# Two-layer attention and expert kernel: paired value products, masked maxima on VectorE, outputs kept transposed, one-piece scratch reads, combine weights repeated by DMA

## The chip, the cores and the metric

One Trainium2 chip, one core. The metric is the device time of one execution in microseconds; the kernel before takes 1240.22 us (median of 3 runs, 1240.1 to 1241.93).

## The reference, cut to what matters

```python
x = L0_attn_x                                   # (1, 1024, 256) float32
xn = _layernorm(x)
s = _L0_attn_ref(xn, ...)                       # differential attention
g = _silu(_L0_ffn_ref(xn, weight, bias))        # MXFP4-rounded x and weight
x = x + s * g
xn = _layernorm(x)
s = _L1_attn_ref(xn, ...)                       # causal attention, 16 heads of 16
g = _silu(_L1_ffn_ref(xn, ...))                 # 16 experts of 176 rows, top 4, and shared rows
x = x + s * g

# L0 attention: 16 heads, 4 key/value heads, two halves of 16
q1, q2 = rope(q halves); k1, k2 = rope(k halves), repeated 4 times
a1 = softmax(q1 k1 / 4 + causal mask); a2 = softmax(q2 k2 / 4 + causal mask)
out = (a1 - lam * a2) @ v                       # v is 32 wide
out = (out - mean) * rsqrt(var + EPS)           # over tokens and the head's 32 columns
out = (out * gn_w + gn_b) * 0.8 @ Wo
# L1 experts
h1 = xt @ W1[e].T; h3 = xt @ W3[e].T
y = sum_e (silu(h1) * h3 * combine[:, e]) @ W2[e].T
```

## The kernel before

Five blocks follow each other, each ended by a barrier of all engines: the setup (lines 175 to 362), the attention of layer 0 (`attention(0, ...)`, L365), `middle` (L798), the attention of layer 1, and `experts` (L1137). All addresses, semaphores and orders are written out by hand; each engine runs its own list in order.

**Setup.** x is normalised, transposed and multiplied by the query and key weights in ten units of 128 rows by 512 tokens (`UN`, L161; keys first). Each unit is rotated (rope) and split into three bf16 parts by ScalarE, VectorE and GpSimd into `spl`, a ring of 4 units; the SP queue writes it to a scratch in DRAM (L221), and `stacked0` (L164) reads it back in six transfers of 16 partitions each, one per pairing of a part of q with a part of k, so that `stack0` holds 96 rows that a single bf16 product contracts. Three more rows hold the row maxima in bf16 parts.

**Attention.** A head, or in layer 1 two heads, is called a pair: 16 pairs in layer 0, 8 in layer 1, each of 24 blocks. For every block TensorE makes three products:
- the max step (L447): scores of 128 queries against up to 512 keys. On the diagonal a second product adds the mask (L451): 16 of the 24. VectorE takes the row maximum out of PSUM (L577, L580). It runs `LEAD` = 38 blocks ahead through a ring of 3 banks.
- the score step (L460): scores of 128 keys against up to 512 queries with the maxima subtracted, into one of `AHEAD` = 2 banks; ScalarE takes the exponential (L535) into `pr`, a ring of 4; GpSimd clears the triangle on the diagonal (L710, 16 of 24).
- the value step (L480): float32, 64 columns of the array in layer 0 and 32 in layer 1. Half m = 0 and half m = 1 of a block pair go to different columns and partitions of one bank. It trails by one block: `value_step(n - 1)`.

The widths (`SB`, L46, and `MB`, L57) add up to 9216 columns in a pair for each of the three. The last column of each value operand is ones, so the sum of the exponentials comes out beside the output. Finished outputs of a pair and 512 tokens are copied by ScalarE (L544), turned by four float32 products with `sel` (L500), copied again (L551), and normalised by VectorE and GpSimd (L598, L690 to L702). SP brings the maxima of the next pair into `stack` (L729), the late units, and in layer 1 the expert weights (L737, L740). In layer 0 VectorE also runs the MXFP4 rounding (L605), one piece of 256 columns per pair in ten pairs.

**Middle.** Group statistics of the layer 0 output, gain and offset (L968, L969), four transposes a tile (L1056), Wo, gate, residual, second norm, transposes, value and router products, then eight projection units of layer 1, split, written and gathered as in the setup (L849, L775), the routing, and the combine weights as three bf16 parts.

**Experts.** 50 units (25 tiles of 128 expert rows, twice for 512 tokens each): 12 products for the two hidden layers (L1237), one with a one-hot matrix that repeats the combine weights over the rows (L1244), ScalarE, VectorE (L1374, L1377, L1383), GpSimd (L1332, L1347, L1351), and two units later 6 products down (L1257). Ahead of them the layer 1 output is transposed (L1212) and multiplied by Wo (L1221); after them eight tiles are transposed back (L1277), gated and stored one by one (L1324, L1389, L1392, L1356, L1202).

## Time and profile before

| | us |
|---|---|
| median of 3 runs | 1240.22 |
| span of the profiled execution (its own time lies about 1.8 above the span, if it is like the median) | 1238.4 |
| TensorE matmul busy | 1135.3 (92%) |
| VectorE busy | 556.6 (45%) |
| ScalarE busy | 478.6 (39%) |
| GpSimd busy | 420.3 (34%) |
| TensorE weight load busy | 496.2 (40%) |

Busy matmul time is modelled and overlaps at its ends, so costs of TensorE are read from one start to the next. "Granted clock" is the share of 2.4 GHz at which TensorE was allowed to run; its two levels are 1.0 (2.4 GHz) and 0.5 (1.2 GHz). PEld is the weight load.

### The profile page before, as it was taken

Reading aid. Unit: us, or ns where it says so; the run is one execution under the profiler, and the core shown is the slowest. Engines: PE = TensorE matmul, PEld = TensorE weight load, DVE = VectorE, ACT = ScalarE, POOL = GpSimd, SP = SyncE. Lnnn points to the kernel's source line nnn. Section 1 sums busy time; section 2 is a strip of 40 time slices with the busy share of each in tenths; the row PEclk is TensorE's granted clock in tenths of the full one; section 3 lists DMA queues with packets and bytes.
Section 4 is the critical chain, followed back from the end, with each engine's and each line's share of the span. In section 5 each row is a group of like instructions: output and inputs, shape, how many; then the busy total and the mean of one; then the engine's idle time right before and its main releaser. Section 6 shows DMA issues by size and latency. Waiting matters only on the chain. (4 is left out here: it accounts for less than half of the span.)

```text
span 1238.4 us, 14306 instructions
## 1 busy us (share of the span) xinstructions
PE 1135.3 (92%) x4490; PEld 496.2 (40%) x4490; DVE 556.6 (45%) x1198; ACT 478.6 (39%) x981; POOL 420.3 (34%) x863
## 2 busy tenths in 40 slices
PE   5559999999999999999797299999999799999996
PEld 2322333333333333333374123222322377777774
DVE  3564555555555444440366264444440044444444
ACT  2313444444444444444223124444444344444443
POOL 2612222222222222222322111222222267767774
PEclk9969999999999999999788679999999899999998
DMA  4755310000000000000103855111111000000001
GB/s 147 146 101 72 47 20 1 1 1 1 1 1 1 1 1 1 1 1 1 30 0 64 141 91 91 40 40 41 40 40 43 24 1 0 0 1 0 0 0 35
DMA packets 32226, 39.24 MB, mean 32 GB/s; under 512 B 5386, under 2 KB 24427, under 8 KB 32158
## 3 DMA queue, kind: packets, MB, share of 16 engines
q1 hardware_dynamic: 32164, 38.48, 15.5%
q8 instruction: 31, 0.51, 0.2%
q14 instruction: 31, 0.25, 0.1%
HBM read 30.05 MB, written 8.13 MB: 31 GB/s over the span
## 5 line engine op out<-in xcount | busy, mean ns | idle before, releaser
L480 PE MATMUL ps<-top,mid 128*64 128x512 f32 (+3 forms) x768 | 330.5, 513 | 0.0
L535 ACT ACTIVATE top<-ps 128x512 f32<-128x512 f32 (+3 forms) x384 | 188.6, 491 | 280.7 <-PE ps L460 280.5
L447 PE MATMUL ps<-mid 96*128 96x512 bf16 (+3 forms) x576 | 194.3, 346 | 46.6 <-DMA mid<-part_scratch 41.3
L580 DVE TENSOR_REDUCE top<-ps 128x1 f32<-128x512 f32 (+3 forms) x256 | 148.7, 587 | 113.0 <-PE ps L447 74.4
L460 PE MATMUL ps<-mid 99*128 99x512 bf16 (+3 forms) x576 | 194.6, 339 | 0.5 <-ACT mid L535 0.3
L460 PEld LDWEIGHTS ps<-mid 99*128 99x128 bf16 x576 | 57.6, 100 | 311.4 <-ACT top L535 191.1
L710 POOL TENSOR_SCALAR_AFFINE_SELECT top<-top 128x128 f32<-128x128 f32 x256 | 74.8, 292 | 251.5 <-ACT top L535 251.5
L480 PE MATMUL ps<-mid 128*32 128x512 f32 (+3 forms) x384 | 159.8, 500 | 0.0
L535 ACT ACTIVATE mid<-ps 128x512 f32<-128x512 f32 (+1 forms) x192 | 94.0, 490 | 152.0 <-PE ps L460 151.5
L1237 PE MATMUL ps<-xp,wp 128*128 128x512 f32 (+1 forms) x600 | 144.7, 390 | 0.0
L1237 PEld LDWEIGHTS ps<-xp,wp 128*128 128x128 f32 (+1 forms) x600 | 111.9, 187 | 24.9 <-issue 0.5
L480 PEld LDWEIGHTS ps<-top,mid 128*64 128x64 f32 x768 | 73.4, 135 | 91.2 <-issue 72.3
L580 DVE TENSOR_REDUCE mid<-ps 128x1 f32<-128x512 f32 (+3 forms) x128 | 73.8, 590 | 55.3 <-PE ps L447 33.8
L577 DVE TENSOR_REDUCE top<-ps 128x1 f32<-128x128 f32 (+3 forms) x128 | 61.1, 483 | 72.1 <-PE ps L451 72.1
L451 PE MATMUL ps<-keep 128*128 128x128 bf16 x384 | 88.2, 230 | 0.0
L1374 DVE SCALAR_TENSOR_TENSOR a<-th,ps 128x512 f32<-128x512 f32 (+1 forms) x50 | 34.4, 687 | 115.5 <-ACT th L1303 115.5
L1332 POOL TENSOR_TENSOR wp<-top,wp 128x512 fp32r<-128x512 f32 (+1 forms) x50 | 64.7, 1295 | 61.7 <-ACT wp L1288 61.7
L1257 PE MATMUL ps<-gp,w2p 128*128 128x512 f32 (+1 forms) x300 | 82.6, 411 | 1.5 <-POOL gp L1351 1.5
L447 PEld LDWEIGHTS ps<-mid 96*128 96x128 bf16 x576 | 58.6, 102 | 62.4 <-issue 42.6
L710 POOL TENSOR_SCALAR_AFFINE_SELECT mid<-mid 128x128 f32<-128x128 f32 x128 | 37.4, 292 | 131.5 <-ACT mid L535 131.5
L1351 POOL TENSOR_TENSOR gp<-g,gp 128x512 fp32r<-128x512 f32 (+1 forms) x50 | 64.1, 1283 | 17.1 <-ACT gp L1316 17.0
L1257 PEld LDWEIGHTS ps<-gp,w2p 128*128 128x128 f32 (+1 forms) x300 | 52.5, 188 | 21.7 <-issue 9.3
(204 smaller groups left out, 1055.7 us busy)
## 6 DMA issues: line engine op xcount, KB each, us to landing
mid<-part_scratch SPq DMA_DIRECT2D x54, 256.0 KB, 9.3
part_scratch<-top SPq DMA_DIRECT2D x18, 384.0 KB, 11.4
top<-in_w SPq DMA_DIRECT2D x16, 396.0 KB, 4.0
top<-in_w SPq DMA_DIRECT2D x8, 384.0 KB, 4.8
keep<-in_x SPq DMA_DIRECT2D x1, 1024.0 KB, 5.8
top<-in_rope SPq DMA_DIRECT2D x1, 1024.0 KB, 7.7
out<-gg SPq DMA_DIRECT2D x8, 128.0 KB, 1.7
mid<-top SPq DMA_DIRECT2D x48, 4.0 KB, 1.7
```

The lines of the kernel that those rows point to most:

```text
L447: ins = nc.tensor.matmul(bank[:, 0:w], queries(pair, m)[0:PARTS, i * P:(i + 1) * P], keys(pair, m)[0:PARTS, c * 512:c * 512 + w], start=Tr ...
L451: ins = nc.tensor.matmul(bank[:, w - P:w], idb[:, :], mkb[:, :], start=False, stop=True)
L460: nc.tensor.matmul(ps[:, ST_BANK + n % AHEAD, 0:w], keys(pair, m)[0:STACK, j * P:(j + 1) * P], queries(pair, m)[0:STACK, q0:q0 + w], start ...
L480: nc.tensor.matmul(ps[r0:r0 + rw, ACC + c, q0 - 512 * c:512], v, pr[:, n % 4, 0:w], start=start, stop=stop).then_inc(multiplied, 1)
L535: nc.scalar.activation(pr[:, n % 4, 0:w], ps[:, ST_BANK + n % AHEAD, 0:w], ACT.Exp, scale=0.25).then_inc(p_ready, 1)
L577: ins = nc.vector.tensor_reduce(nm[:, pair % 2, m, i:i + 1], bank, AX.X, ALU.max, negate=True)
L580: ins = nc.vector.tensor_reduce(mx[:, m, i - 4, c:c + 1], bank, AX.X, ALU.max)
L710: nc.gpsimd.affine_select(out=square, in_=square, pattern=[[1, P]], compare_op=ALU.is_ge, fill=0.0, base=0, channel_multiplier=-1).then_in ...
L1237: last = nc.tensor.matmul(ps[0:r, bank + b, :], wp[:, b, pw, w + kk, 0:r], xp[:, px, kk, c * 512:(c + 1) * 512], start=j == 0 and kk == 0, ...
L1257: last = nc.tensor.matmul(ps[:, YB + kk, :], w2p[0:r, b, pw, kk * P:(kk + 1) * P], gp[0:r, b, pg, :], start=first and j == 0, stop=final a ...
L1332: nc.gpsimd.tensor_tensor(wp[:, b, 1, :, 0:r], w13[:, :, :, bass.ds(i * P, r)].rearrange("p w c n -> p (w c) n"), wp[:, b, 0, :, 0:r].bitc ...
L1351: nc.gpsimd.tensor_tensor(gp[0:r, b, 1, :], g[0:r, b, :], gp[0:r, b, 0, :].bitcast(F32), ALU.subtract).then_inc(gl_ok, 1)
```

## The change

What it does, by place (line numbers with "after" are those of the changed kernel):
- Value steps are issued in groups: the two halves of a block together (`GROUPS`, 12 groups in a pair in layer 0), in layer 1 from block 8 on four together, each on its own 32 columns. The rings grow: 3 score banks, `pr` of 8.
- The mask product is gone. VectorE adds the mask and takes the maximum in one operation that also writes the masked scores back to PSUM, with the maximum read out by a second small instruction (L709 after).
- The products with `sel` and their copies are gone. Outputs stay transposed in `oT`: SP moves them from the copied bank into `oT` (halves apart in layer 0) and the sums of exponentials into `cd` (L435 after); for every four pairs VectorE inverts, SP writes the inverses to DRAM and reads them repeated, GpSimd multiplies, VectorE combines the halves and takes statistics.
- The scratch holds each unit six times in the order of the stack, written in three transfers, and is read in one transfer of 96 partitions, the first two maps of a group ahead of the other six. `spl` has 8 units.
- MXFP4 runs in five pieces of 512 columns, six of eleven steps on GpSimd.
- Middle: no transposes of the output; gain and offset act on `oT` in place; the bias row is bf16 in three parts; units in another order; combine weights go to DRAM in float32.
- Experts: no transposes ahead, no one-hot product; two DMAs a unit repeat rows of the combine weights; Wo products run inside the sweep; tiles 0 to 3 are turned and gated inside the sweep; the last copy is shared by two engines.

```diff
-                S_RING, AHEAD = 3, 2
+                RING, LAG = 8, 1
+                GROUPS = [(b, b + 2) for b in range(0, 8 if not first else PAIR, 2)]
+                if not first:
+                    GROUPS += [(b, b + 4) for b in range(8, PAIR, 4)]
+                GROUP_AT = {(hi + LAG) % PAIR: (lo, hi) for lo, hi in GROUPS}
+                S_RING, AHEAD = 3, 3
...
-                            if diag:
-                                ins = nc.tensor.matmul(bank[:, w - P:w], idb[:, :], mkb[:, :], start=False, stop=True)
...
-                            if n > 0:
-                                value_step(n - 1)
...
-                            if out_number(n) >= 0:
-                                sel_step(out_number(n), pair + 1)
+                            if k in GROUP_AT and n > LAG:
+                                lo, hi = GROUP_AT[k]
+                                for done in range(n - LAG - (hi - lo), n - LAG):
+                                    value_step(done)
...
+                            if c == i // 4:
+                                low = i < 4
+                                to = nm[:, pair % 2, m, i:i + 1] if low else mx[:, m, i - 4, c:c + 1]
+                                ins = nc.vector.tensor_tensor_reduce(
+                                    bank, bank, msk[:, 512 - w:512], -1.0 if low else 1.0,
+                                    3e38 if low else -3e38, ALU.add, ALU.min if low else ALU.max, to)
```

```diff
-            for n, j in enumerate(KPARTS if f == 4 else QPARTS):
-                sp.dma_start(stack0[16 * n:16 * n + 16, base:base + 8, :],
-                             scr[j, f * P:(f + 1) * P, :].rearrange("(m r) t -> r m t", r=16)).then_inc(stk0[f], 16)
+            sp.dma_start(stack[0:PARTS, at + lo:at + hi, :],
+                         of[f * P + 16 * lo:f * P + 16 * hi, :, :].rearrange("(m r) n t -> (r n) m t", r=16)
+                         ).then_inc(done, 16)
...
+            def outputs(sp, pair, c):
...
+                    for m, to in ((0, o1[32 * h:32 * h + 32, f, columns(c)]), (1, second(f)[32 * h:32 * h + 32, c, :])):
+                        at, row = 64 * m, 16 * (2 * h + m)
+                        sp.dma_start(to, src[at:at + 32, :]).then_inc(outs[c], 16)
+                        sp.dma_start(cd[row:row + 16, c, 0, :], src[at + 32:at + 33, :]).then_inc(outs[c], 16)
...
+            def scale(pool, f, c):
...
+                pool.wait_ge(inv_r[c], READS * (f + 1))
+                if first:
+                    n1, rd = second(f)[:, c, :], repeated(c)
+                    nc.gpsimd.tensor_tensor(n1, n1, rd[1], ALU.mult)
+                    nc.gpsimd.tensor_tensor(to, to, rd[0], ALU.mult).then_inc(scaled, 1)
...
+                        for pair in range(N):
+                            if pair > 0:
+                                outputs(sp, pair - 1, 1)
+                            if f > 0 and h == 0:
+                                inverses(sp, f - 1, 0)
+                            if pair + 1 < N:
+                                ahead(pair + 1)
+                            outputs(sp, pair, 0)
+                            if f > 0 and h == 0:
+                                inverses(sp, f - 1, 1)
...
-                    nc.tensor.matmul(ps[0:r, CB + b, :], ones[:, bass.ds(i * P, r)], combT(c),
-                                     start=True, stop=True).then_inc(c_ok, 1)
...
+                    if c == 0 and isinstance(i, int) and 3 <= i < 4:
+                        for q in range(2):
+                            through_wo(q)
```

How the order moves, at two places. TensorE in layer 0, from the middle of a pair on; L447 is the max step, L451 the mask, L480 the value step, L460 the score step. Before:

```order
L447 MATMUL ps<-mid 128x512
L451 MATMUL ps<-keep 128x128
L480 MATMUL ps<-top,mid 64x512
L460 MATMUL ps<-mid 128x512
L447 MATMUL ps<-mid 128x128
L451 MATMUL ps<-keep 128x128
L480 MATMUL ps<-top,mid 64x512
L460 MATMUL ps<-mid 128x512
L447 MATMUL ps<-mid 128x128
```

and now, where L622 is the score step, L605 the max step and L642 the value step ("x2" is two in a row):

```order
L622 MATMUL ps<-mid 128x512
L605 MATMUL ps<-mid 128x128
L622 MATMUL ps<-mid 128x512
L605 MATMUL ps<-mid 128x128
L642 MATMUL ps<-top,mid 33x512 x2
L622 MATMUL ps<-mid 128x512
L605 MATMUL ps<-mid 128x256
```

Two value products now stand together behind two score and two max steps, and the mask products are gone.

VectorE in layer 0, now (L709 is the masked maximum and its read-out, L713 the plain maximum, L717 the join of the halves, L725 the copy of the maxima rows):

```order
L713 TENSOR_REDUCE top<-ps 128x1
L709 ISA ps,top<-ps,keep 128x512
L709 ISA top 128x1
L717 TENSOR_REDUCE top<-top 128x2x4
L709 ISA ps,top<-ps,keep 128x128
L709 ISA top 128x1
L709 ISA ps,top<-ps,keep 128x128
L709 ISA top 128x1
L709 ISA ps,top<-ps,keep 128x256
L709 ISA top 128x1
```

Sixteen of the 24 maxima of a pair became two instructions each, of which the first has two inputs and writes a whole block.

## Rows read from the trace of the kernel before

**Rows 1.** Stretches: us, busy PE, PEld, DVE, ACT, POOL, granted clock, DMA share, GB/s.
```profile
72.00:93.00 21.00, 16.94 (x73) 6.91 (x73) 18.16 (x41) 1.58 (x3) 1.63 (x7) 0.66 0.32 75
93.00:603.00 510.00, 507.58 (x1993) 167.82 (x1991) 231.58 (x533) 210.09 (x445) 134.65 (x441) 1.00 0.07 9
604.00:706.00 102.00, 68.66 (x274) 43.90 (x275) 51.00 (x168) 25.62 (x55) 26.89 (x33) 0.75 0.38 65
706.00:727.00 21.00, 17.88 (x74) 7.16 (x74) 18.49 (x41) 1.88 (x4) 1.75 (x7) 0.58 0.29 60
727.00:970.00 243.00, 242.94 (x951) 70.66 (x951) 91.32 (x183) 102.57 (x220) 50.88 (x183) 1.00 0.22 52
```

**Rows 2.** TensorE in layer 0, in order of time: start, us, line, shape.
```profile
281.07 0.22 PE L447 MATMUL ps<-mid 96*128 96x128 bf16 x1
281.13 0.22 PE L451 MATMUL ps<-keep 128*128 128x128 bf16 x1
281.27 0.86 PE L480 MATMUL ps<-top,mid 128*64 128x384 f32 x2
282.07 0.23 PE L460 MATMUL ps<-mid 99*128 99x128 bf16 x1
...
283.51 0.65 PE L480 MATMUL ps<-top,mid 128*64 128x256 f32 x2
```

**Rows 3.** Groups of the other engines and of the `sel` products: busy us, mean ns.
```profile
L535 ACT ACTIVATE top<-ps 128x512 f32<-128x512 f32 (+3 forms) x384 | 188.6, 491 | 280.7 <-PE ps L460 280.5
L500 PE MATMUL ps<-keep,top 128*128 128x66 f32 x256 | 35.4, 281 | 0.7 <-ACT top L544 0.7
L241 POOL TENSOR_TENSOR top<-top 128x512 f32<-128x512 f32 x10 | 14.5, 1452 | 15.1 <-DVE top L315 15.1
```

**Rows 4.** TensorE at the end of each attention, where two value products meet.
```profile
598.24 0.65 PE L480 MATMUL ps<-top,mid 128*64 128x256 f32 x4
...
968.74 0.63 PE L480 MATMUL ps<-mid 128*32 128x256 f32 x4
```

**Rows 5.** VectorE, in order of time: a maximum and what follows it; two operations with PSUM.
```profile
280.05 0.69 DVE L580 TENSOR_REDUCE top<-ps 128x1 f32<-128x512 f32 x1 [0.74 <-PE ps L447]
280.65 0.41 DVE L637 TENSOR_TENSOR top<-top 128x256 f32<-128x256 f32 x1
...
995.71 0.69 DVE L1374 SCALAR_TENSOR_TENSOR a<-th,ps 128x512 f32<-128x512 f32 x1 [2.70 <-ACT th L1303]
996.43 0.69 DVE L1377 TENSOR_TENSOR a<-a,ps 128x512 f32<-128x512 f32 x1
```

**Rows 6.** Waits for scratch, in order of time; then GB/s in 40 slices: gathers, unit writes.
```profile
59.62 0.62 ACT L270 CAST top<-top 128x512 bf16<-128x512 f32 x1 [11.78 <-DMA part_scratch<-top]
72.24 0.26 PE L447 MATMUL ps<-mid 96*128 96x128 bf16 x1 [19.64 <-DMA mid<-part_scratch]
705.91 0.27 PE L447 MATMUL ps<-mid 96*128 96x128 bf16 x1 [21.63 <-DMA mid<-part_scratch]
GB/s 0 0 7 7 7 92 266 120 113 126 130 109 102 137 109 106 113 157 109 109 113 140 92 99 157 109 41 0 27 0 0 0 0 0 0 0 0 0 0 0
GB/s 0 0 0 0 0 106 352 357 337 357 313 29 0 0 0 0 0 0 0 0 5 299 357 337 357 337 159 0 0 0 0 0 0 0 255 352 352 347 347 198
```

**Rows 7.** TensorE in the experts, in order of time: Wo, first hidden products, one whole unit.
```profile
982.13 10.14 PE L1221 MATMUL ps<-wo_s,oT 128*128 128x256 f32 x32 [6.97 <-DMA onehot_s<-in_onehot]
...
998.56 3.02 PE L1237 MATMUL ps<-xp,wp 128*128 128x512 f32 x12
...
1003.32 2.88 PE L1237 MATMUL ps<-xp,wp 128*128 128x512 f32 x12
1006.13 0.39 PE L1244 MATMUL ps<-keep,onehot_s 51*128 51x512 bf16 x1
1006.45 1.66 PE L1257 MATMUL ps<-gp,w2p 128*128 128x512 f32 x6
1007.95 0.39 PE L1237 MATMUL ps<-xp,wp 128*128 128x512 f32 x1
```

More of the change, by code:

```diff
@@ new lines, in program, with unit_written, written @@
+        unit_near = sem("unit_near")
+        scr_ok = [sem(f"scr_{n}") for n in range(SLOTS)]
+        def unit_written(layer, v):
+            slot = v % SLOTS
+            before = len(range(slot, len(UN), SLOTS)) if layer == 1 else 0
+            return scr_ok[slot], 48 * (before + v // SLOTS + 1)
+        UN = [(f, c) for f in (4, 0, 1, 2, 3) for c in range(NC)]
+        UN1 = [(2, 0), (0, 0), (2, 1), (0, 1), (3, 0), (1, 0), (3, 1), (1, 1)]
+        def written(sp, to, f, c, parts, is_key, done):
+            rows = to[f * P:(f + 1) * P, :, c * 512:(c + 1) * 512]
+            for first_row, width, part in ((0, 3, 0), (3, 2, 1), (5, 1, 2)):
+                if is_key:
+                    of = parts[:, part, :].unsqueeze(1).to_broadcast([P, width, 512])
+                else:
+                    of = parts[:, 0:width, :]
+                sp.dma_start(rows[:, first_row:first_row + width, :], of).then_inc(done, 16)
@@ new lines, in attention @@
+            o_evac = sem(f"o_evac{layer}")
+            outs = [sem(f"outs{layer}_{c}") for c in range(NC)]
+            inv, inv_w, scaled = (sem(f"{n}{layer}") for n in ("inv", "inv_w", "scaled"))
+            inv_r = [sem(f"inv_r{layer}_{c}") for c in range(NC)]
+            combined = sem("combined0") if first else scaled
+            if not first:
+                den_sum, num_sum = sem("den_sum"), sem("num_sum")
+            PER = (64, 64) if first else (64, 128)
+            READS = 32 if first else 16
@@ L649, in _ @@
                             pair, k = divmod(n, PAIR)
+                            f, h = divmod(pair, 4)
                             if n + LEAD < BLOCKS:
@@ L741, in weights, with ahead @@
                                          ).then_inc(ld_m, 16)
-                        for pair in range(N):
+                        def ahead(pair):
                             rows(pair)
@@ L1069, in _, with ffn @@
                 last.then_inc(q_tr, 1)
-                for n, part in enumerate((pm, pq)):
+                pe.wait_ge(q_ev, 3)
+                pe.wait_ge(bip_ok, 2)
+                def ffn(t):
+                    z = ps[:, 4 + t // 2, (t % 2) * D:(t % 2 + 1) * D]
+                    for k in range(KD):
+                        nc.tensor.matmul(z, aT[:, k, t * P:(t + 1) * P], wT[:, k, :], start=k == 0, stop=False)
+                    for j in range(3):
+                        last = nc.tensor.matmul(z, row[:, :], bip[:, j, :], start=False, stop=j == 2)
+                    last.then_inc(f_mm, 1)
@@ L1071, in _, with total @@
+                def total(n):
                     pe.wait_ge(stats, n + 1)
-                    nc.tensor.matmul(ps[:, 7, 16 * n:16 * n + 16], share[:, :], part[:, :], start=True,
+                    nc.tensor.matmul(ps[:, 3, 4 * n:4 * n + 4], share[:, :], (pm, pq)[n][:, :], start=True,
                                      stop=True).then_inc(tot, 1)
+                for t in range(NT):
+                    ffn(t)
+                    if t >= 6:
+                        total(t - 6)
                 def values(t):
-                    pe.wait_ge(ldw, 64)
@@ L1222, in _, with back @@
                                                     wo1[:, k, :], start=k == 0, stop=k == KD - 1)
                     last.then_inc(s_mm, 1)
-                pe.wait_ge(xl_ok, 1)
+                def back(t, bank, at):
+                    for k in range(KD):
+                        last = nc.tensor.transpose(ps[:, bank, at + k * P:at + (k + 1) * P],
+                                                   yT[:, t // 4, k, (t % 4) * P:(t % 4 + 1) * P], idf[:, :])
+                    last.then_inc(z_ok, 1)
```

973 lines of the change are left out of this document (553 added, 420 removed).

## The prediction

> **What bounds the kernel now.** I read the busy time by stretches first, to see which engine fills which stage. In both steady attention stretches TensorE is full: 507.58 of 510 us and 242.94 of 243 us, at granted clock 1.00, with VectorE at 45% and 38% [rows 1]. So 753 of 1238 us cost what TensorE's instructions cost. The two short stretches ahead of them (21 us each) belong to VectorE: it is busy 18.2 and 18.5 us there, and the clock is 0.66 and 0.58. The middle has TensorE at 67%.
>
> Next I read TensorE's instructions in order, from one start to the next. A max product of 128 columns takes 0.06 us (281.07 to 281.13), the mask product behind it and the switch to the value product 0.14, so a mask costs about 0.07. A value product of 384 columns takes 0.80 to the next score product (281.27 to 282.07) [rows 2]. At 2.4 GHz one bf16 pass is 384/2400 = 0.16 us; 0.80 is 384/600 = 0.64 plus 0.16. With the 0.08 on its front, a value product costs w/600 us and 0.245 us fixed. Each kind of product has 9216 columns and 24 instructions a pair:
>
> - value 15.36 + 24 x 0.245 = 21.2 us
> - score 3.84 + 24 x 0.01 = 4.1; max 4.1; 16 masks 1.1
> - `sel`: 35.4 us busy for 16 pairs, 2.2 each [rows 3]
>
> Sum 32.7; measured 510/16 = 31.9, so the model is right to 3%.
>
> **Side by side.** At the end of the layer 0 attention two value products of 256 columns that have nothing between them, one per half of the array, lie in one group that lasts 0.65 us; in layer 1, on 32 columns each, 0.63 [rows 4]. One product alone of the same width lasts 0.65 [rows 2]. So two cost one; that they do is no hope but a row. That four cost one is shown by no row. I take it, since layer 1 shows two products on quarter tiles; if four cost two rounds, that is a bound below.
>
> Layer 0 after: values 7.68 + 12 x 0.245 = 10.7 (a group costs its fixed part once), score 4.1, max 4.1: 18.9 a pair, 302 in all, less 38 max products that run in the stretch ahead (6 us): 296. Layer 1: four groups of two (512, 384, 256, 128 columns: 0.853 + 0.640 + 0.427 + 0.213) and four groups of four (3 x 0.853 + 0.427) are 5.1 us, with 8 x 0.245 = 7.1; with score and max 15.3 a pair, 122 in all, less 6: 116.
>
> **Who could be late instead.** ScalarE: 24 exponentials at 0.491 are 11.8 us a pair by duration [rows 3], and two copies make some 13, less from start to start. GpSimd: all its work in layer 0 is 134.65/16 = 8.4 a pair [rows 1]; the scaling adds, each four pairs, 4 operations of 1.45 [rows 3], 1.5 a pair. VectorE: a maximum of 512 columns takes 0.60 from start to start and 0.69 by duration [rows 5]; all 24 are w/960 + 0.07 each, 11.3 a pair. The masked maximum is on no row. Bounds: nothing more than a plain maximum (it reads the same bank), or 0.6 more at 512 (as if adding and taking the maximum were two passes). The nearest rows are operations of the same engine with PSUM on one side and 512 elements of output, 0.69 each, 0.72 when the second depends on the first [rows 5]; with the read-out behind it I take 0.2 more per masked block: 11.3 + 3.2 = 14.5. That is below 18.9 in layer 0 and just below 15.3 in layer 1.
>
> So layer 0 keeps TensorE as its bound with 77% for VectorE there; I add 12 us for MXFP4 pieces of 512 columns on VectorE and steps of GpSimd among its triangles, a stall of 0.5 to 1 us a pair. Layer 1 has three engines within 20%; rows of maxima that SP brings while the next max products are already due add some 0.7 to 1 us a pair, and uneven load 3 to 5: 14 in all. Both stretches ahead, 38 maxima with VectorE as bound, grow by about 38 x 0.13 = 5 us each. Sums: layer 0 from 508 (its 510 and the last steps) to 308, -200; layer 1 from 243 to 130, -113.
>
> **Start.** ScalarE stood 11.78 us for the ring of 4 units, TensorE 19.64 us for the gather, which moved 102 to 126 GB/s, while unit writes move 350 [rows 6]. The ring of 8 takes the first wait; the read in one transfer of 96 partitions and the near maps first take most of the second. The scratch is written twice as large (six copies for three): at 350 GB/s a unit of 786 KB needs 2.2 us, about one unit's pace of GpSimd (2.8). I put the first max product at 56.5 for 72.24: -15.7. If the wide read gave nothing, +10.
> The Trainium skill (page "SBUF — State Buffer", on how partitions reach the DMA ports) says that a transfer confined to partitions 0 to 15 reaches 4 ports and measured 104 GB/s. By that rule, the gathers of before agree with it (102 to 126), and a transfer of 96 partitions should not be held so.
>
> **Middle.** TensorE's wait of 21.63 before layer 1 [rows 6] shrinks to some 5, for the same reasons and by the order of the units: -17. Four transposes and their copies for each of eight tiles go, -7, the rest of the tile loop stays. Sum -24; -14 to -32 as bounds.
>
> **Experts.** Before: the first hidden products of the second unit at 998.56, 28.6 us after the last value product; a unit takes 4.63 us (1003.32 to 1007.95), of which the one-hot product has 0.32 (1006.13 to 1006.45), 0.55 with its two switches [rows 7]. I take 0.42 x 50 = -21. The transposes ahead and the wait for the one-hot matrix (6.97 us) go, the inverses of the last heads, their trip through DRAM and the scaling now stand before Wo but not before the hidden products: -9. Wo takes 10.14 us there, partly at half clock; inside the sweep 8: +8. The last tiles, four turned inside the sweep at 1.1 each: -4.6. Two issues of SP per unit, within 4.2 us, cost nothing while both land in time: each reads one row of 2 KB and writes 128 partitions. If they don't, a unit waits (+1 here; up to +20 as bound). Sum -25.5.
>
> **Sum**, against the profiled execution: 1238.4 - 15.7 + 5 - 200 - 24 + 5 - 113 - 25.5 = 870, and 1.8 for what lies around the span (the median stands 1.8 above it): **871 us**. Of the 368 us saved, 310 are the value products, `sel` and masks.
>
> **Rivals.**
> (a) VectorE sets the pace. The masked maximum costs its upper bound (0.6 more at 512, 0.37 on average, and the read-out): 17.3 us or more a pair. Layer 1 then follows it (+16 to +20), layer 0, where VectorE has MXFP4 too, +10, both stretches ahead +8 each: about 915. TensorE would then idle a tenth of layer 1, and the rows say what idling can do: in the stretches where it waits between products its granted clock is 0.58 and 0.66 [rows 1]. At 1.2 GHz layer 1's 15.3 us become some 25, +80 less what VectorE costs anyway: up to 950. For it: 14.5 against 15.3 is close. Chance 0.14.
> (b) Four cost two rounds, or the products meet only in part because operands come late: layer 1 pays 3 x 0.853 + 0.427 again, +3 us a pair, 24 in all: 895. This lies inside the likeliest range, so it is counted there.
> (c) Products keep strict turns. A float32 product is two instructions on the trace; if the first of a neighbour could not start before the second of the other had started, only one pass in three would be shared. A pair of layer 0 would take 3/4 of the old value time instead of half, +3.84 x 16 = 61; in layer 1 five passes for eight instead of two, +5.5 x 8 = 44: 976. [Rows 4] speak against it: x4 in 0.65 us, not 0.97. Chance 0.04.
> The Trainium skill (page "TensorE: Matmul & The Clock Gate", Part 3, on packing small matmuls) states that matmuls start and end strictly in program order. By that rule two neighbours of two passes would share one pass only, which is this rival; the trace speaks against it.
> (d) The value products don't meet at all in the steady state (both halves share a bank and a stationary load that blocks): only the switches are saved. +7.7 x 16 and +10 x 8 come back: about 1075. Chance 0.03.
> (e) Slower than before: the masked maximum, one instruction with two inputs and a written block, is dear. VectorE would need (1240 - 360)/24, over 34 us a pair where it now needs 11.3, so 1.8 us for an average masked block of 320 columns. No row comes near: 0.69 for 512, and even GpSimd's 1.45 for 512 would give about 970. Chance 0.01. That the change does not do what it says I can exclude but for such costs: the new order shows the products next to each other.
>
> **How the numbers follow.** My forecast (TensorE sets the pace, both widths side by side) has 0.78 with its own range of 832 to 905; its spread is +-12 for start and middle, -15 to +24 for layer 1, +-15 for layer 0 stalls, -12 to +20 for the experts, which don't all fall to one side. (a) 0.14 at 905 to 950, (c) 0.04 at 976, (d) 0.03 at 1075, (e) 0.01. A range of 832 to 950 leaves out (c), (d), (e) and an edge of the first. A difference under 0.2%, 2.5 us, can't be told from none for this kernel; all cases but (e) are far beyond it. Faster 0.985, same 0.005, slower 0.01.
>
> **What would show it.** First max product near 56; stretches ahead 26 us each with VectorE full; layer 0's steady part 308 us with TensorE over 90% busy at clock 1.00, VectorE 77%; groups of value products 0.86 us for 512 columns in x4, and x8 in layer 1; the masked maximum at 0.7 to 0.9 us for 512; middle 78 us; layer 1 130 us; experts 243. Wrong if masked maxima last over 1.1 us, if TensorE waits mostly for VectorE (a), if x4 groups last 1.3 (c) or 1.7 (d), if x8 lasts 1.7 (b), or if the granted clock leaves 1.00 in either attention.

## The result and the profile after

The changed kernel takes **868.4 us** (median of 4 runs, 865.64 to 868.93) against 1240.16 us in the same comparison: ratio 0.6998, 95% interval 0.6986 to 0.701. The forecast was 871, its range 832 to 950. The profiled execution has a span of 867.2 us.

The first view is again the stretches, now of the changed kernel, with cuts at the first max product, the first score product and the last value product of each layer. Columns: us, busy PE, PEld, DVE, ACT, POOL, granted clock, DMA share, GB/s.

```profile
0.00:63.70 63.70, 34.36 (x108) 18.16 (x109) 29.57 (x63) 21.33 (x38) 30.34 (x30) 0.94 0.64 200
63.70:82.00 18.30, 14.62 (x39) 4.23 (x40) 17.48 (x65) 0.00 (x0) 0.96 (x6) 0.50 0.22 67
82.00:375.00 293.00, 291.70 (x1514) 84.02 (x1512) 209.42 (x653) 184.92 (x415) 133.77 (x358) 0.99 0.19 47
375.00:470.50 95.50, 60.71 (x248) 37.95 (x249) 40.51 (x152) 24.45 (x51) 22.37 (x35) 0.76 0.38 106
470.50:488.80 18.30, 14.63 (x39) 4.22 (x40) 17.49 (x65) 0.00 (x0) 1.10 (x6) 0.50 0.28 92
488.80:623.00 134.20, 126.14 (x738) 35.79 (x736) 88.00 (x277) 88.60 (x207) 46.13 (x159) 0.94 0.40 112
623.00:867.00 244.00, 220.75 (x950) 180.61 (x948) 126.95 (x170) 112.99 (x211) 195.92 (x160) 0.94 0.22 63
```

With the kernel before cut at the same events (72.2, 90.3, 599.2, 705.9, 724.0 and 969.7 us), the forecast can be set beside the measured change stage by stage:

| stage | before | after | change | forecast |
|---|---|---|---|---|
| start to first max product | 72.2 | 63.7 | -8.5 | -15.7 |
| stretch ahead, layer 0 | 18.1 | 18.2 | +0.1 | +5 |
| layer 0, first score to last value | 508.9 | 292.9 | -216.0 | -200 |
| middle | 106.7 | 95.8 | -10.9 | -24 |
| stretch ahead, layer 1 | 18.1 | 18.2 | +0.1 | +5 |
| layer 1 | 245.7 | 134.0 | -111.7 | -113 |
| experts | 268.7 | 244.5 | -24.2 | -25.5 |
| sum | 1238.4 | 867.2 | -371.2 | -368 |

The sum was right to 3 us, but five of the seven terms were not: the start and the middle gave 20 us less than forecast, VectorE's two stretches and layer 0 gave 26 us more. That the total came so close was partly luck; the two large terms, the layers with 313 of the 368 us forecast, were read from the right rows.

The next rows are in order of time: two value products of 512 columns and their neighbours in layer 0, then four in layer 1. "x4" is two products of two passes, "x8" four.

```profile
372.09 0.34 PE L622 MATMUL ps<-mid 99*128 99x256 bf16 x2
372.36 1.05 PE L642 MATMUL ps<-top,mid 128*33 128x512 f32 x4
373.34 0.23 PE L622 MATMUL ps<-mid 99*128 99x128 bf16 x1
...
619.50 0.28 PE L622 MATMUL ps<-mid 99*128 99x256 bf16 x1
619.71 1.05 PE L642 MATMUL ps<-mid 128*17 128x512 f32 x8
620.70 0.34 PE L622 MATMUL ps<-mid 99*128 99x256 bf16 x2
```

Both groups last 1.05 us, and the next score product comes 0.98 and 0.99 us after their start. By the w/600 of the prediction the 512 columns of one product, in its two passes, are 0.853 us. So two products cost one, as [rows 4] had shown, and four cost one too, which no row had shown. In the group of four the first passes start within 0.02 us of each other, at 619.71 to 619.73, and the second passes 0.44 us later. The four extra weight loads are hidden as well.

VectorE at the start of the stretch ahead, where it sets the pace (L709 is the masked maximum, its second row the read-out):

```profile
64.24 0.33 DVE L709 CUSTOM_DVE_ANT_0 ps<-ps,keep 128x128 f32<-128x128 f32 x1
64.48 0.14 DVE L709 DVE_READ_ACCUMULATOR2_ANT top<- 128x1 f32 x1
64.48 0.47 DVE L709 CUSTOM_DVE_ANT_0 ps<-ps,keep 128x256 f32<-128x256 f32 x1
...
66.28 0.73 DVE L709 CUSTOM_DVE_ANT_0 ps<-ps,keep 128x512 f32<-128x512 f32 x1
66.93 0.73 DVE L709 CUSTOM_DVE_ANT_0 ps<-ps,keep 128x512 f32<-128x512 f32 x1
67.58 0.69 DVE L713 TENSOR_REDUCE top<-ps 128x1 f32<-128x512 f32 x1
```

A masked maximum of 512 columns takes 0.65 us from start to start (66.28 to 66.93) against 0.60 for a plain one in [rows 5]. The read-out runs inside the next instruction. The first eight maxima, two of each width, take 3.56 us (64.02 to 67.58); in the kernel before the same eight, plain, took 3.45:

```profile
706.32 3.53 DVE L577 TENSOR_REDUCE mid<-ps 128x1 f32<-128x128 f32 x8 [14.26 <-PE ps L451]
709.77 1.48 DVE L580 TENSOR_REDUCE mid<-ps 128x1 f32<-128x512 f32 x3
```

So the mask costs VectorE 0.01 to 0.05 us a block, where 0.2 was taken. (The eight plain ones are from the stretch ahead of layer 1; ahead of layer 0 they take 3.44.)

### The profile page after: what moved, and what is told of

The parts are those of the page before. It is cut to its first block and busy times, and to the rows that moved or that the text cites. A ratio compares the mean times of both kernels' runs of the same rounds, so it can differ in the third digit from the quotient of the medians.

```text
span 867.2 us, 12855 instructions
## 1 busy us (share of the span) xinstructions
PE 762.9 (88%) x3632; PEld 365.0 (42%) x3632; DVE 529.4 (61%) x1441; ACT 432.3 (50%) x922; POOL 430.6 (50%) x751
## 5 line engine op out<-in xcount | busy, mean ns | idle before, releaser
L675 ACT ACTIVATE top<-ps 128x512 f32<-128x512 f32 (+3 forms) x384 | 171.0, 490 | 132.4 <-PE ps L622 132.2
L605 PE MATMUL ps<-mid 96*128 96x512 bf16 (+3 forms) x576 | 191.2, 356 | 29.0 <-PEq L981 11.8
L709 DVE CUSTOM_DVE_ANT_0 ps<-ps,keep 128x512 f32<-128x512 f32 (+3 forms) x384 | 184.2, 504 | 41.9 <-PE ps L605 41.2
L622 PE MATMUL ps<-mid 99*128 99x512 bf16 (+3 forms) x576 | 185.7, 338 | 9.2 <-ACT mid L675 6.3
L642 PE MATMUL ps<-top,mid 128*33 128x512 f32 (+3 forms) x768 | 161.6, 500 | 0.0
L622 PEld LDWEIGHTS ps<-mid 99*128 99x128 bf16 x576 | 54.3, 99 | 185.8 <-ACT top L675 103.0
L675 ACT ACTIVATE mid<-ps 128x512 f32<-128x512 f32 (+1 forms) x192 | 82.6, 492 | 69.9 <-PE ps L622 41.8
L713 DVE TENSOR_REDUCE top<-ps 128x1 f32<-128x512 f32 x128 | 88.4, 691 | 36.0 <-PE ps L605 35.5
L605 PEld LDWEIGHTS ps<-mid 96*128 96x128 bf16 x576 | 58.2, 102 | 75.3 <-issue 30.1
L1533 ACT CAST gp<-g 128x512 fp32r<-128x512 f32 (+1 forms) x50 | 31.1, 622 | 68.3 <-DVE g L1631 68.3
L1568 POOL TENSOR_TENSOR w2p<-top,w2p 128x256 fp32r<-128x256 f32 (+1 forms) x50 | 57.5, 1151 | 2.7 <-ACT w2p L1530 2.7
L642 PE MATMUL ps<-mid 128*17 128x512 f32 (+3 forms) x384 | 55.0, 512 | 0.0
L713 DVE TENSOR_REDUCE mid<-ps 128x1 f32<-128x512 f32 x64 | 44.1, 689 | 16.2 <-PE ps L605 16.1
```

Of the source, the lines that this page charges most:

```text
L605: nc.tensor.matmul(ps[:, s_bank(turn), 0:w], queries(pair, m)[0:PARTS, i * P:(i + 1) * P], keys(pair, m)[0:PARTS, c * 512:c * 512 + w], st ...
L622: nc.tensor.matmul(ps[:, ST_BANK + n % AHEAD, 0:w], keys(pair, m)[0:STACK, j * P:(j + 1) * P], queries(pair, m)[0:STACK, q0:q0 + w], start ...
L642: nc.tensor.matmul(ps[r0:r0 + dv, ACC + c, q0 - 512 * c:512], v, pr[:, n % RING, 0:w], start=start, stop=stop).then_inc(multiplied, 1)
L675: nc.scalar.activation(pr[:, n % RING, 0:w], ps[:, ST_BANK + n % AHEAD, 0:w], ACT.Exp, scale=0.25).then_inc(p_ready, 1)
L709: ins = nc.vector.tensor_tensor_reduce(bank, bank, msk[:, 512 - w:512], -1.0 if low else 1.0, 3e38 if low else -3e38, ALU.add, ALU.min if ...
L713: ins = nc.vector.tensor_reduce(mx[:, m, i - 4, c:c + 1], bank, AX.X, ALU.max)
```

## Where the start and the middle lost what was forecast

The change takes ScalarE's wait for the ring of 4 away, and GpSimd has finished its last unit at 56.2 us, which is where the forecast put the first max product. It starts at 63.70. SP, in order of time:

```profile
46.37 0.82 SPq L182 DMA_DIRECT2D mid<-part_scratch  x2
47.23 15.85 SPq L178 DMA_DIRECT2D part_scratch<-top  x18
```

SP issues 18 unit writes until 63.08, 0.88 us each, and the block of the setup ends for all engines only when SP's list is done. While it does so the DMA engines are full:

```profile
52.00:56.00 4.00, 0.67 (x6) 0.47 (x5) 0.87 (x2) 2.83 (x6) 3.87 (x4) 1.00 1.07 289
56.00:60.00 4.00, 0.00 (x0) 0.00 (x0) 0.35 (x2) 0.00 (x0) 0.18 (x1) 0.55 1.09 383
60.00:64.00 4.00, 0.28 (x3) 0.31 (x4) 0.00 (x0) 0.00 (x0) 0.26 (x2) 0.50 1.09 384
```

The same stands at the end of the middle: 12 writes issued from 456.60 on take SP 13.03 us, and TensorE waits 11.76 us for the end of the block. Besides, the outputs' last part costs more there than the transposes gave back: the tile loop starts 28.8 us after the block's first product (378.83 to 407.67), for 19.6 before, since the inverses of the last heads go through DRAM first: GpSimd waits for them until 396.86. Without the transposes a tile then takes 2.95 us from start to start for 3.74, 6.3 in eight tiles.

```profile
396.86 1.26 POOL L491 TENSOR_TENSOR top<-top 128x512 f32<-128x512 f32 x1 [12.33 <-DMA top<-inverse_scratch]
401.78 0.59 PE L1231 MATMUL ps<-top 128*128 128x4 f32 x2 [7.01 <-DVE top L1122]
...
407.67 7.27 PE L1273 MATMUL ps<-top,keep 128*128 128x256 f32 x24 [3.59 <-ACT keep L1041]
...
470.51 1.86 PE L605 MATMUL ps<-mid 96*128 96x128 bf16 x7 [11.76 <-PEq L981]
```

Two theories could explain SP's 0.88 us an issue: full DMA engines, whose queue lets SP add work only as fast as work leaves, or the issues as such. The next two runs tell them apart.

## Experiments

Ratios below are to the kernel before in the same comparison, with 95% intervals; the changed kernel has 0.6986 to 0.701.

**One piece more in every unit write.**

```diff
-            for first_row, width, part in ((0, 3, 0), (3, 2, 1), (5, 1, 2)):
+            for first_row, width, part in ((0, 2, 0), (2, 1, 0), (3, 2, 1), (5, 1, 2)):
```

> The changed kernel with each unit written in four transfers for three, the same bytes. If DMA bandwidth holds SP at the end of the setup and of the middle: no change in either (within 1 us). If the issues of SP do (15.85 us for 18 DMAs, 0.88 each): six units behind the gathers cost 6 x 0.88 = 5 us in the setup and about as much in the middle, 868 + 10 = 878.

Measured: 868.05 us (867.41 to 869.73), ratio 0.7001 (0.6989 to 0.7013). First max product at 64.1 for 63.7, the middle 96.1 for 95.8. SP now:

```profile
46.97 16.47 SPq L178 DMA_DIRECT2D part_scratch<-top  x24
```

24 issues in 16.47 us for 18 in 15.85: 0.69 each for 0.88. The bytes set the pace, not the issues: that is the first theory. (From run to run, with the setup unchanged, the first max product comes at 63.1 to 65.2 us, so 0.4 us there says nothing; the 18 writes take 15.6 to 16.0 in all of them.)

**The far gather behind the writes.**

```diff
                         if u == 3:
                             near_maps0(sp, 0)
-                            far_maps0(sp, 0)
+                    far_maps0(sp, 0)
```

> The changed kernel with the 1152 KB gather of the far maps of the first group issued after the last unit write of the setup instead of ahead of six of them. Theory 1 (the setup's end waits for SP, and SP for DMA bandwidth: the trace shows 380 to 385 GB/s until the barrier): 1.15 MB leave the way of the writes, the first max product comes 3 us earlier, 60.7 for 63.7, and the far maps are needed only by the second pair, some 12 us later: 865. Theory 2 (SP is held by its own issues, 0.88 us each): one issue less ahead, at most 0.9 us earlier. Rival: the second pair's first max product waits for the gather, nothing gained.

Measured: 867.57 us (866.96 to 868.54), ratio 0.6995 (0.6986 to 0.7005). The first max product comes at 62.7, 1.0 us earlier, not 3, and that is within its spread; the writes themselves are the measure:

```profile
47.41 13.98 SPq L178 DMA_DIRECT2D part_scratch<-top  x18
61.43 0.68 SPq L182 DMA_DIRECT2D mid<-part_scratch  x1
```

The writes are issued 1.7 us sooner (61.39 for 63.08), and 0.7 of it goes to issuing the gather, still inside the block. That 1.15 MB at 380 GB/s give only 1.7 us back and not 3 was missed; with the gather behind, the engines run at 366 GB/s from 52 to 56 us and 347 from 56 to 60, which would fit that GpSimd's making of units now holds the writes in part; no run tests it. A gain of 0.8 us in the median can't be told from none.

**Value steps one at a time.**

```diff
-                GROUPS = [(b, b + 2) for b in range(0, 8 if not first else PAIR, 2)]
-                if not first:
-                    GROUPS += [(b, b + 4) for b in range(8, PAIR, 4)]
+                GROUPS = [(b, b + 1) for b in range(PAIR)]
```

> The changed kernel with value steps one at a time again (24 groups of one in a pair), all else kept. Theory (products side by side save a whole block's columns and the fixed part once a group): a pair's value products go from 10.7 to 15.36 + 24 x 0.245 = 21.2 us in layer 0 (+169 over 16 pairs) and from 7.1 to 21.2 in layer 1 (+113 over 8, less the 18 us in which TensorE now waits there): 1130 to 1150 us. Rival (the gain came from masks, sel and the transposed outputs, the grouping is worth its switches alone): 868 + 24 x 3 = 940 at most.

Measured: 1115.15 us (1114.88 to 1115.42), ratio 0.8993 (0.8968 to 0.9017): 247 us given back, 15 less than the low end of what was expected. Value products, layer 0 and layer 1, with the first and last start after the comma; first of the changed kernel, then of this one:

```profile
L642 PE MATMUL ps<-top,mid x768: 272/552/1065, 85.7 to 374.7; 128*33 128x512 f32 x96, 128*33 128x384 f32 x32, 128*33 128x256 f32 x32, 128*33 128x128 f32 x32
L642 PE MATMUL ps<-mid x384: 272/546/1061, 492.5 to 622.6; 128*17 128x512 f32 x96, 128*17 128x384 f32 x32, 128*17 128x256 f32 x32, 128*17 128x128 f32 x32
```

```profile
L640 PE MATMUL ps<-top,mid x768: 272/552/1063, 85.6 to 536.9; 128*33 128x512 f32 x96, 128*33 128x384 f32 x32, 128*33 128x256 f32 x32, 128*33 128x128 f32 x32
L640 PE MATMUL ps<-mid x384: 272/546/1061, 651.8 to 870.2; 128*17 128x512 f32 x96, 128*17 128x256 f32 x33, 128*17 128x384 f32 x32, 128*17 128x128 f32 x31
```

Layer 0: 451.3 us for 289.0, +162 (169 expected). Layer 1: 218.4 for 130.1, +88, below the 95 to 113 expected. The durations of single records are the same in both kernels: nothing in a record tells that its product shares its time, only the starts do. The rival, 940 at most, is out.

**The grouping alone, in the kernel before.**

```diff
-                            if n > 0:
-                                value_step(n - 1)
+                            if n > 0 and n % 2 == 0:
+                                value_step(n - 2)
+                                value_step(n - 1)
```

with a ring of 6 for `pr` and the last two steps behind the loop.

> The kernel before with one edit: value steps two at a time, every second block, in both layers, with a ring of 6 exponentials for 4. Theory (the same sum): 10.6 us a pair less on TensorE, 24 pairs: 1240 - 254 = 986. Rival 1 (rings too short: TensorE waits for exponentials behind each group): 1020 to 1080. Rival 2 (products of two passes share one pass only): 3.84 us a pair less than that gain, 1240 - 254 + 92 = 1078.

Measured: 993.25 us (992.68 to 993.83), ratio 0.801 (0.7987 to 0.8032); 246 us less, by 254 expected. Layer 0 went from 508.9 to 339.3 us (first score to last value), 169.6 less, which is 16 x 10.6; layer 1 from 245.7 to 165.9, 80 of the 85 expected. Both rivals, short rings and one shared pass in three, are out. The value operands still have their 64 and 32 columns here, so the 33 and 17 of the changed kernel are not what the gain hangs on. This single edit is two thirds of the whole gain.

**Groups of two in all of layer 1.**

```diff
-                GROUPS = [(b, b + 2) for b in range(0, 8 if not first else PAIR, 2)]
-                if not first:
-                    GROUPS += [(b, b + 4) for b in range(8, PAIR, 4)]
+                GROUPS = [(b, b + 2) for b in range(0, PAIR, 2)]
```

> The changed kernel with groups of two in layer 1 from block 8 on as well. TensorE then needs 19.3 us a pair in layer 1 for 15.3. Theory 1 (four side by side cost one, and layer 1 now loses 18 us to waits that a slower TensorE would hide): +14 us, 882. Theory 2 (the waits add to TensorE's time whatever it does): +32, 900. Rival (four side by side cost two rounds already, or another engine sets layer 1's pace): no change.

Measured: 876.78 us (875.92 to 878.51), ratio 0.7071 (0.7053 to 0.7089): +8.4 us. Layer 1 takes 143.6 for 134.0. TensorE's own sum for it by the rule is 8 x 19.3 - 6 = 148, 4 us too much. With groups of four the rule gives 116 and the time is 134. Of these 18 us the trace gives 8.1 as idle time of TensorE (134.20 us less 126.14 busy); with groups of two it is 0.6:

```profile
488.90:632.40 143.50, 142.88 (x738) 38.11 (x736) 89.81 (x278) 91.64 (x207) 46.29 (x159) 0.98 0.37 104
```

So a slower TensorE does hide the idle time, and the rival (four already cost two rounds) is out. Theory 1 holds, at two thirds of its size. Another 7 us are the price of 14.7 us at the low clock, where groups of two have 6.5 us of it; the section on the forecast has the rows.

**The mask back on TensorE.**

```diff
+                            if diag:
+                                ins = nc.tensor.matmul(ps[:, s_bank(turn), w - P:w], idb[:, :], msk[:, 384:512], start=False, stop=True)
...
-                                ins = nc.vector.tensor_tensor_reduce(
-                                    bank, bank, msk[:, 512 - w:512], -1.0 if low else 1.0,
-                                    3e38 if low else -3e38, ALU.add, ALU.min if low else ALU.max, to)
+                                ins = nc.vector.tensor_reduce(to, bank, AX.X, ALU.max, negate=low)
```

> The changed kernel with the mask product on TensorE and plain maxima on VectorE, as in the kernel before. Theory (TensorE is the bound of both attentions, the masked maximum costs VectorE only some 0.04 us over a plain one): 16 x 0.07 = 1.1 us a pair on TensorE, 27 us over 24 pairs, and 2 to 3 us in each of the two stretches ahead, where TensorE runs at 1.2 GHz: 893 to 900. Rival (the masked maximum is dear and VectorE paces layer 1): 0.13 x 16 us a pair come back there, and the time stays within 5 us of 868.

Measured: 880.95 us (878.16 to 884.21), ratio 0.71 (0.7072 to 0.7128): +12.6, half of what was expected. Layer 0 takes 305.2 for 292.9 us. Of the 256 masks 229 lie there (27 fall on the 38 blocks that run ahead), so one costs 12.3/229 = 0.054 us, which is 128 columns at 2.4 GHz and nothing for the switch; 0.07 had been read. Layer 1 takes 2.9 us more (136.9 for 134.0) where its 101 masks would be 5.4. That its waits cover the rest is not shown: layer 1 unchanged takes 131 to 134 us from run to run. The stretches ahead stay at 18.1 and 18.7 us.

**The masked maximum alone, in the kernel before.**

```diff
-                            if diag:
-                                ins = nc.tensor.matmul(bank[:, w - P:w], idb[:, :], mkb[:, :], start=False, stop=True)
...
+                            if c == i // 4:
+                                low = i < 4
+                                to = nm[:, pair % 2, m, i:i + 1] if low else mx[:, m, i - 4, c:c + 1]
+                                ins = nc.vector.tensor_tensor_reduce(
+                                    bank, bank, msk[:, 512 - w:512], -1.0 if low else 1.0,
+                                    3e38 if low else -3e38, ALU.add, ALU.min if low else ALU.max, to)
```

> The kernel before with the mask product replaced by the masked maximum alone. Theory (TensorE is the bound, a mask costs it the 0.053 us that putting it back into the changed kernel cost): 15 masks a pair in the steady part x 24 pairs x 0.053 = 19 us less: 1221; the stretches ahead of it unchanged, since VectorE needs 0.04 us more for a block and TensorE has slack there. By the 0.07 of the prediction: 1213. Rival (dear maxima on VectorE): the steady part is unchanged and the two stretches ahead grow by 5 us each: 1250.

Measured: 1222.36 us (1219.26 to 1223.15), ratio 0.9846 (0.9829 to 0.9863): 17.7 us less, by 19 expected from 0.053 (the 19 counted 15 masks a pair; 330 lie in the two layers, 13.75 a pair, which makes 17.5). Layer 0 495.4 for 508.9, layer 1 241.1 for 245.7, both stretches ahead 18.2.

**More work on VectorE.**

```diff
                             turn = in_turn(n)
+                            for e in range(3):
+                                nc.vector.memset(idle[:, 3 * k + e, :], 0.0)
```

> The changed kernel with three memsets of 128x8 on VectorE in front of every maximum, as a stand-in for a masked maximum that is dearer (0.07 to 0.12 us each, by 32x32 memsets of 0.12 in the trace: 0.2 to 0.36 a block, 5 to 8.6 us a pair). If VectorE's slack is what the busy times say (layer 0: 13.1 of 18.3 us a pair, layer 1 in the full pairs 13.4 of 16): both stretches ahead +8 to +14 each, layer 0 +0 to +40, layer 1 +16 to +35: 895 to 960. The rival of the prediction also has TensorE's clock fall to 1.2 GHz in layer 1 when VectorE sets the pace: then layer 1 takes over 190 us. If there is more slack than busy times say, only the two stretches ahead grow: 885 to 890.

Measured: 871.13 us (870.28 to 872.0), ratio 0.7022 (0.7011 to 0.7033): +2.7. The load was too light to decide what it was meant to: three memsets cost 0.042 us a block from start to start (both stretches ahead grew from 18.2 to 19.8, 1.6 us for 38 blocks), not 0.2 to 0.36, for they overlap. Small work shows by its duration (65 ns each) more than it costs. Layer 0 (294.2) and layer 1 (132.7) stay within what they take unchanged (292.9 to 294.3 and 131 to 134), so they have at least 1 us a pair of slack on VectorE, which is what the load comes to. What a masked maximum dearer by 0.37 would have done, the clock included, stays open.

**Expert weights behind the outputs.** In layer 1 one wait stands out, in the second pair:

```profile
517.12 0.58 ACT L685 COPY mid<-ps 64x512 f32<-64x512 f32 x1 [2.48 <-DMA keep<-mid]
...
518.24 0.61 PE L622 MATMUL ps<-mid 99*128 99x512 bf16 x1 [2.76 <-ACT mid L675]
```

ScalarE's copy of a finished output waits until SP's transfers have emptied the copy's target; they had been issued from 505.95 us on, behind 1.2 MB of expert weights (504.35 to 505.91). TensorE stood 2.76 us, and its granted clock fell from 1.00 to 0.61 in the ten us around it:

```profile
515.00:525.00 10.00, 7.24 (x31) 1.71 (x29) 4.60 (x20) 4.22 (x8) 2.05 (x8) 0.61 0.15 22
525.00:535.00 10.00, 10.00 (x58) 2.98 (x56) 6.69 (x19) 5.88 (x16) 3.41 (x12) 0.88 0.38 129
```

```diff
                             rows(pair)
                             late(sp, pair)
-                            if not first:
-                                weights(pair)
...
                             outputs(sp, pair, 0)
+                            if not first and pair + 1 < N:
+                                weights(pair + 1)
```

> The changed kernel with the expert weights of layer 1 (1.2 MB for a pair) issued by SP behind the outputs of a pair instead of ahead of them. Theory (in the second pair ScalarE's copy waits 2.48 us for small output transfers that are queued behind these bytes, TensorE then stands 2.76 us and its granted clock falls, 0.61 from 515 to 525 us): that wait goes, and with it the low clock, 5 to 8 us in all: 861 to 863, with the clock at 1.00 from 500 us on. Rival (SP as a whole is late in the second pair, its 12 output issues of 0.6 us each): the wait only moves, no gain.

Measured: 865.47 us (864.54 to 867.0), ratio 0.698 (0.697 to 0.699): 2.9 us less. Layer 1 itself takes 128.2 us for 134.0, 5.8 less, and the wait and the low clock are gone:

```profile
515.00:525.00 10.00, 9.79 (x64) 2.87 (x63) 8.59 (x30) 6.67 (x16) 3.12 (x12) 1.00 0.42 126
```

The 5.8 us are not all the price of that wait. Five other runs keep it (the split write, the late far gather, the ring of 9, the load on VectorE, GpSimd's order): it is 2.4 to 2.9 us there, but the clock stays low for 3 to 7 us behind it, not 10, and layer 1 takes 131 to 133 us. Against those, taking the wait away is worth 3 to 5 us.

In this execution layer 0 took 296.4 us where the changed kernel took 292.9 and the other variants with the same layer 0 took 293.1 to 294.3. The trace shows why: TensorE waited for rows of maxima, and then ran at the low clock for some 7 us. First this run, then the changed kernel, where the same wait was 1.29 us and the clock stayed up:

```profile
323.69 0.38 PE L622 MATMUL ps<-mid 99*128 99x512 bf16 x1 [1.94 <-DMA mid<-top]
325.00:335.00 10.00, 10.00 (x40) 2.58 (x38) 5.50 (x14) 4.92 (x11) 4.39 (x10) 0.66 0.21 66
```

```profile
325.00:335.00 10.00, 10.00 (x57) 3.08 (x56) 7.97 (x23) 7.35 (x16) 5.11 (x12) 1.00 0.22 66
```

So the stage confirms the theory, and the whole time, 2.9 us less in the median, shows the low end of it.

**One more slot in layer 1's ring.**

```diff
-                RING, LAG = 8, 1
+                RING, LAG = 8 if first else 9, 1
```

> The changed kernel with 9 exponentials for 8 in layer 1's ring (there is no room for more). In layer 1 ScalarE stood 27.5 us in 30 waits for value products that free a slot. Theory (these waits make the 21 us that layer 1 loses against TensorE's own sum of 113): one slot is half an exponential of slack in each of 32 groups of four, 3 to 8 us less: 861 to 865. Rival (ScalarE's idle time costs nothing, TensorE's loss comes from SP and from the ends of stages): within 1.5 us of 868.

Measured: 867.65 us (865.53 to 870.36), ratio 0.7001 (0.6989 to 0.7014). Layer 1 132.1 us, within the 131 to 134 of the runs that leave it alone. Not to be told from none: the rival holds, or one slot is too little. ScalarE's 27.5 us of waits for value products were not the price they looked like.

**GpSimd's order at the start of the experts.**

```diff
                 low_w13(1, 1, 1)
-                env["last_scaled"](pool)
-                pool.wait_ge(xh_ok, 2)
...
+                env["last_scaled"](pool, (0,))
...
+                    if c == 0 and isinstance(i, int) and i == 0:
+                        env["last_scaled"](pool, (1,))
```

and the rounding rest of the second half of the tokens behind unit 22. In the changed kernel TensorE waited at the third unit for GpSimd, which had waited for the inverses and then done the rest that nobody needed yet:

```profile
640.01 1.26 POOL L494 TENSOR_TENSOR keep<-keep 128x512 f32<-128x512 f32 x1 [2.98 <-DMA keep<-inverse_scratch]
641.23 2.39 POOL L1560 TENSOR_TENSOR xp<-keep,xp 128x1024 fp32r<-128x1024 f32 x1
...
645.35 5.32 PE L1450 MATMUL ps<-xp,wp 128*128 128x512 f32 x12 [5.54 <-POOL wp L1552]
```

> The changed kernel with two GpSimd operations of the start of the experts moved into the sweep: the scaling of the last 512 tokens behind the first unit's weights, the rounding rest of the second half of the tokens (2.39 us, needed after 25 units) behind unit 22. In the changed kernel GpSimd stood 2.98 us for the inverses and TensorE 5.54 us for GpSimd at 645 us. Theory (GpSimd's order at the start holds TensorE, and later it has slack, 3.9 of 4.05 us a unit): 3 to 5 us less, 863 to 865. Rival (GpSimd is the bound through the sweep): only its own idle time comes back, 0 to 1 us, since the moved work is paid later.

Measured: 863.16 us (862.66 to 863.69), ratio 0.6959 (0.695 to 0.6969): 5.2 us less, all kept to the end (last value product to end 239.2 us for 244.5).

```profile
639.21 3.00 PE L1450 MATMUL ps<-xp,wp 128*128 128x512 f32 x12 [0.46 <-DVE g L1634]
```

GpSimd has slack in the sweep, if little: 42.36 of 50 us there, and the sweep itself got faster by more than forecast. One stretch of 50 us of the kernel before, then of the changed one:

```profile
1050.00:1100.00 50.00, 50.00 (x206) 36.58 (x206) 21.92 (x33) 23.27 (x44) 35.15 (x34) 1.00 0.00 0
```

```profile
700.00:750.00 50.00, 50.00 (x222) 41.19 (x221) 26.20 (x36) 24.08 (x46) 42.36 (x36) 1.00 0.20 61
```

From start to start a unit of the sweep takes 4.08 us (822.17 to 826.25) for 4.63: 0.55 saved, the upper of the two bounds.

**All four edits together.**

> Four edits of the changed kernel together: far gather behind the setup's writes, expert weights behind the outputs, 9 slots in layer 1, GpSimd's two operations in the sweep. If they act in different stages and none is given back, the gains add: 868.4 - 1 - 3 - (0 to 5) - (0 to 5) = 855 to 864.

Measured: **856.57 us** (854.77 to 857.29), ratio 0.6906 (0.6895 to 0.6917), 11.8 us below the changed kernel. The single gains were 0.8, 2.9, 0.8 and 5.2, 9.7 in sum, so the gains add within the spread of the runs; the first max product is at 61.5, layer 1 takes 127.3 us. This version beats both kernels.

## Why the forecast was right, and where its steps were not

- **What bounds the kernel, and side by side**: right. The rule of w/600 + 0.245 us gives 296 us for layer 0 in its steady part (308 with the stalls added to it), 292.9 were measured. The row with two products [rows 4] carried 250 us of the forecast, and the run with the grouping alone shows it.
- **Four cost one**: taken without a row; right, 1.05 us for x4 and x8.
- **12 us of stalls in layer 0** ("a stall of 0.5 to 1 us a pair"): this step failed. TensorE has one gap over 0.25 us in all of it, of 1.29. MXFP4 pieces on VectorE were covered; 209.42 us busy of 293 left room for them.
- **Masked maximum at +0.2, stretches ahead +5 each**: failed, 0.01 to 0.05 and +0.1. The nearest row was right (0.69 for an operation with PSUM on one side; the masked maximum, with PSUM on both, lasts 0.69 to 0.73 at 512 columns); the extra for the read-out was wrong, because start to start it is hidden in the next instruction. The step added a duration where a start-to-start distance was due.
- **Mask product 0.07**: 0.054, a size.
- **Start -15.7**: failed by 7.2. "About one unit's pace of GpSimd" compared a unit's write (2.2 us) with a unit's making (2.8) and left out that gathers of 1.9 MB share the bandwidth, and that the block ends only when SP has issued everything. What was missing is a sum of bytes between the first unit and the barrier.
- **Middle -24**: failed by 13, for the same reason (the wait is 11.8, not some 5: 7 us) and since the last outputs' trip through DRAM now stands ahead of the tile loop (9 us), which the sum placed only in the experts. The transposes came out at 6.3 for 7, and some 4 us that nobody had forecast came back in the rest of the block.
- **Layer 1 -113**: -111.7; the 14 us put on top of TensorE's 116 for rows and imbalance were 18, but made of other things. TensorE is idle for 8.1 us: 2.8 in the one wait for ScalarE's copy, 1.0 in all for rows of maxima (0.7 to 1 a pair had been put), the rest in waits of 0.7 us and less, most of them for exponentials. And it runs at 1.2 GHz for the first 4.5 us of the layer and for 10.2 behind the one wait, which is worth some 7 us and stood nowhere in the sum. Some 3 us are left open.

```profile
488.80:493.30 4.50, 4.50 (x14) 1.44 (x14) 3.17 (x10) 2.88 (x7) 2.05 (x7) 0.50 1.06 240
517.20:527.40 10.20, 9.16 (x34) 2.44 (x35) 4.24 (x15) 5.29 (x12) 2.17 (x8) 0.50 0.30 90
```

- **Experts -25.5**: -24.2. One-hot product -28 for -21, but 5.5 us of TensorE's wait for GpSimd at the third unit, which was nowhere in the sum. A reading was off, too: 998.56 in [rows 7] is the third unit, not the second (the first two start at 991.93 and 995.29). From the last value product to the third unit the changed kernel takes 22.7 us for 28.9.
- **Rivals**: (a) did not happen: no maximum is on the bound outside the stretches ahead. But one of the signs of being wrong did show: the granted clock left 1.00 in layer 1 (0.94 over the layer, 0.61 in ten us), behind a wait for a transfer and not for VectorE. (b), (d) are out by the rows and by both grouping runs. (c), that products take strict turns so that one pass in three is shared, is out: the columns of an x4 group would take 1.28 us and those of an x8 group 2.13, and from start to start both take under 1.0. (The 0.97 that the prediction gives this rival at 256 columns is too much: one more pass is 0.21 on top of 0.65, 0.86.) The Trainium skill (page "TensorE: Matmul & The Clock Gate", Part 3, on packing small matmuls) says that matmuls start and end strictly in program order; the trace does not bear that out for products of two passes on different columns of the array: in the x8 group above all four first passes start before any second one, though the kernel issues the products one after another.

## What to carry to other kernels

Further products with few output columns cost nothing when they run beside the first, on other columns of the array: look in the old trace for a place where two happen to meet, since one such row priced two thirds of this gain. Price an added instruction by start to start, never by its duration, and before a barrier add up the bytes that all queues still have to move, because the queue that issues them ends last. After the big term is gone, look for single waits of 2 to 5 us on TensorE in order of time: here two of them, both caused by the order of another engine's list, were worth 8 us.

## What the runs showed of the hardware that was not expected

- Four float32 products on 17 columns each take the time of one (1.05 us at 512 columns for x8).
- A maximum that also adds a mask and writes the masked block back to PSUM costs 0.65 us at 512 columns, 0.05 more than the plain one.
- Behind a wait of 2.76 us of TensorE its granted clock was 0.61 in ten us. Taking the wait away was worth 5.8 us in the layer against this execution and 3 to 5 against five others, in which the clock came back sooner after nearly the same wait.
- In layer 0 a granted clock of 0.66 in ten us followed a wait of 1.94 us, in one execution out of those shown.
- SP's issue time stretches to 0.88 us a transfer when the DMA engines run at 380 GB/s, and is 0.69 when the same bytes go in 24 transfers for 18.
